# New orders of the work in four phases instead of three, with transpositions placed behind each run of small matmul tiles and each bfloat16 product

## What is computed

```python
x = x + _L0_xattn_ref(_layernorm(x), ctx, ctx, ...)   # 16 heads of 8, softmax over 64 keys
x = x + _L0_ffn_ref(_layernorm(x), ...)               # 8 experts, top 2: relu(x W1 + b1) W2 + b2, weighted
x = x + _L1_xattn_ref(_layernorm(x), ctx, ctx, ...)   # attention without biases
x = x + _L1_ffn_ref(_layernorm(x), ...)
# the last one: c = sigmoid(.) * c + sigmoid(.) * tanh(.) over the 128 sequences as time steps,
# then h = tanh(xt @ wo.T + c_final @ uo.T + bo)
```

## Time and profile before

| | us |
|---|---|
| median of three runs | 842.12 (841.3 to 842.35) |
| the profiled execution | 841.05 |
| its span | 839.2 |
| busy in the span: TensorE matmuls | 820.6 |
| ScalarE | 775.4 |
| VectorE | 775.3 |
| GpSimd | 682.5 |

### The profile page before, as it was taken

How to read it: one execution, slowest core, us unless ns; L and a number is a source line. 1 busy time by engine, 2 the same in 40 slices (tenths; PEclk the granted TensorE clock), 3 DMA queues, 4 the chain that set the end, 5 groups by cost and what they waited for, 6 DMA issues and landing times.

```text
span 839.2 us, 42592 instructions
## 1 busy us (share of the span) xinstructions
PE 820.6 (98%) x15268; PEld 743.5 (89%) x15268; DVE 775.3 (92%) x2778; ACT 775.4 (92%) x2490; POOL 682.5 (81%) x1292
## 2 busy tenths in 40 slices
PE   8899999999999999999999999999999999999996
PEld 5688999999999999999999999999999999998884
DVE  6789999999999999999999999999999999999855
ACT  5899999999999999999999999999999999998874
POOL 5888998888888888888888888888888888887644
PEclk7999999999999999999999999999999999999999
DMA  9400000000000000000000000000000000000005
GB/s 345 175 3 3 2 4 4 4 3 4 3 3 4 4 4 3 4 3 4 3 4 4 4 4 4 3 3 4 3 4 3 4 3 4 4 4 3 3 3 201
DMA packets 6969, 17.74 MB, mean 21 GB/s; under 512 B 752, under 2 KB 2288, under 8 KB 6768
## 3 DMA queue, kind: packets, MB, share of 16 engines
q1 hardware_dynamic: 6336, 14.36, 4.5%
q10 hardware_dynamic: 432, 0.68, 0.3%
HBM read 10.84 MB, written 4.19 MB: 18 GB/s over the span
## 4 chain that ended last, share of the span: by engine, by line
PE 90%; DVE 4%; ACT 3%; issue 2%; POOL 1%; DVEq 0%; POOLq 0%; ACTq 0%
PE ps L458 15%; PE ps L480 13%; PE ps L393 13%; PE ps L378 8%; PE ps L423 7%; PE ps L554 6%; PE ps L540 5%; PE ps L329 4%; PE ps L358 4%; PE ps L437 3%; PE ps L343 3%; PE ps L320 2%; PE ps L404 2%; PE ps L321 2%; PE ps L493 1%
## 5 line engine op out<-in xcount | busy, mean ns | idle before, releaser
L1512 POOL TENSOR_TENSOR h<-Ex 128x512 f32<-128x512 f32 (+1 forms) x144 | 165.9, 1152 | 57.6 <-issue 51.2
L1106 DVE TENSOR_REDUCE mx<-ps 128x8 f32<-128x512 f32 (+1 forms) x288 | 167.0, 620 | 8.2 <-PE ps L378 7.9
L1120 DVE TENSOR_TENSOR Ex<-ps,mx 128x512 f32<-128x512 f32 (+1 forms) x288 | 170.8, 617 | 0.1
L819 ACT ACTIVATE ET<-ps 128x512 f32<-128x512 f32 (+1 forms) x288 | 166.0, 584 | 3.2 <-PE ps L393 2.9
L808 ACT ACTIVATE Ex<-Ex 128x512 f32<-128x512 f32 (+1 forms) x288 | 165.1, 608 | 2.0 <-DVE Ex L1120 1.8
L393 PE MATMUL ps<-w,Ex 128*128 128x128 f32 x1024 | 158.8, 275 | 0.1
L1212 DVE SCALAR_TENSOR_TENSOR acc<-ps,we,acc 128x128 f32<-128x128 f32 x448 | 147.9, 330 | 1.3 <-issue 0.2
L458 PEld LDWEIGHTS ps<-xT,w 128*128 128x128 f32 x1024 | 124.2, 191 | 24.6 <-issue 24.6
L458 PE MATMUL ps<-xT,w 128*128 128x128 f32 x1024 | 144.9, 284 | 0.0
L857 ACT ACTIVATE hT<-ps,w 128x128 f32<-128x128 f32 x512 | 140.1, 398 | 3.1 <-PE ps L458 2.8
L480 PE MATMUL ps<-w,hT 128*128 128x128 f32 x1024 | 139.0, 279 | 0.0
(11 more groups left out here) (108 smaller groups left out, 1847.4 us busy)
## 6 DMA issues: line engine op xcount, KB each, us to landing
cx<-ctx_dram SPq DMA_DIRECT2D x7, 512.0 KB, 12.5
x<-x_dram SPq DMA_DIRECT2D x7, 512.0 KB, 13.1
out_dram<-x SPq DMA_DIRECT2D x14, 256.0 KB, 2.7
w<-weights_dram SPq DMA_DIRECT2D x2, 512.0 KB, 5.4
w<-weights_dram SPq DMA_DIRECT2D x1, 576.0 KB, 8.7
out_dram<-x SPq DMA_DIRECT2D x4, 128.0 KB, 2.6
w<-weights_dram ACTq DMA_DIRECT2D x1, 328.0 KB, 4.4
w<-weights_dram ACTq DMA_DIRECT2D x1, 256.0 KB, 3.1
```

The lines of the kernel that those rows point to most:

```text
L819: e.activation(ET[:, j % 2, r, lo:hi, :, :], b[:, 256 * lo:256 * hi].rearrange("p (c w q) -> p c w q", c=hi - lo, w=2), ACT.Copy).then_inc ...
L1106: e.tensor_reduce(mx[:, j % 2, r, 4 * lo:4 * hi], b[:, 256 * lo:256 * hi].rearrange("p (j k) -> p j k", k=64), AX.X, ALU.max).then_inc(sig ...
L1120: e.tensor_tensor(Ex[:, j % 2, r, 256 * lo:256 * hi].rearrange("p (j k) -> p j k", k=64), b[:, 256 * lo:256 * hi].rearrange("p (j k) -> p ...
L1512: e.tensor_tensor(u, v[:, :, :, 0:32], v[:, :, :, 32:64], ALU.add).then_inc(sig("half1"), 1)
```

## The change

All lags, phases, bank tables and orders are new. There are four phases (rounds -1 to 5, 6 to 11, 12 to 65, 66 to 79) instead of three (0 to 14, 15 to 71, 72 to 79). No operation is added or taken away on any engine, and no shape is changed. VectorE has more waits for its own earlier results (`mv`, `D0` to `D3`, `ri`, `tix`), since the new order would otherwise let a buffer be written anew too soon. `EVEN` is the tile from which empty instructions are strewn between TensorE's products.

```diff
-EVEN = 2
+EVEN = 3
...
-STARTS = (0, 15, 72)
+STARTS = (-1, 6, 12, 66)
...
-       "y1": 3, "e2": 4, "gate": 1, "q": 2, "rt": 4, "turnw": 2, "h0": 2, "sB": 2, "S": 2, "h1": 2, "xin": 1,
+       "y1": 3, "e0": 4, "gate": 1, "turnw": 2, "e1": 4, "h0": 2, "sB": 2, "S": 2, "rt": 4, "h1": 2, "xin": 1,
...
+AHEAD = {"sA": (0, -2, 0, 0), "pv": (1, 0, 0, 0), "e2": (0, 0, 0, -1), "wx0": (4, 3, 2, 0), "q": (0, 0, 0, -1),
...
                     e.wait_ge(sig(f"in_x{chunk[t]}"), 16)
+                if t >= 2:
+                    e.wait_ge(sig("mv"), t - 1)
                 e.bn_stats(st[:, t % 2, 0, :], x[:, t, :]).then_inc(sig("st0"), 1)
...
                 e.wait_ge(sig("xa"), j + 1)
+                if j + L1 >= 2:
+                    e.wait_ge(sig("mv"), j + L1 - 1)
...
                 e.wait_ge(sig("xm"), t + 1)
+                e.wait_ge(sig("mv"), t + L2 - 1)
...
                 e.wait_ge(sig(f"S{r}"), j + 1)
+                if j >= 2:
+                    e.wait_ge(sig(f"D{r}"), j - 1)
...
                 e.wait_ge(sig("half2"), 2 * (j + 1))
+                if j >= 2:
+                    e.wait_ge(sig("ri"), j - 1)
...
                 e.wait_ge(sig("gate"), t + 1)
+                if t >= 2:
+                    e.wait_ge(sig("tix"), t - 1)
```

More of the change, by code:

```diff
@@ L110, in due @@
 def due(i, name):
-    ahead = AHEAD.get(name, (0, 0, 0))
+    ahead = AHEAD.get(name, (0, 0, 0, 0))
     done = max(r + ahead[phase(r)] for r in range(i - 48, i))
@@ L564, in tensor_program @@
                     project_bias()
+                for r in due(i, "y1"):
+                    experts(r, 1)
+                for r in due(i, "e1"):
+                    turn_e(r, 1)
+                for r in due(i, "e3"):
+                    turn_e(r, 3)
+                for r in due(i, "h1"):
+                    hidden(r, 1)
+                for r in due(i, "sB"):
+                    step(r, 1)
+                for r in due(i, "p"):
+                    project(r)
+                for r in due(i, "turnw"):
+                    turn_w(r)
@@ new lines, in tensor_program @@
+                for r in due(i, "wx0"):
+                    out_inputs(r, 0)
+                for r in due(i, "q"):
+                    query(r)
+                for r in due(i, "wx1"):
+                    out_inputs(r, 1)
+                for r in due(i, "gate"):
+                    gate(r)
+                for r in due(i, "sA"):
+                    step(r, 0)
+                for r in due(i, "e2"):
+                    turn_e(r, 2)
+                for r in due(i, "y0"):
+                    experts(r, 0)
@@ new lines, in tensor_program @@
+                for r in due(i, "e0"):
+                    turn_e(r, 0)
+                for r in due(i, "S"):
+                    scores(r)
+                for r in due(i, "turnx"):
+                    turn_x(r)
+                for r in due(i, "xin"):
+                    cell_inputs(r)
+                for r in due(i, "rt"):
+                    turn_r(r)
+                for r in due(i, "kv"):
+                    keys_values(r)
+                for r in due(i, "h0"):
+                    hidden(r, 0)
@@ L937, in scalar_program @@
                     turn_w(r)
+                for r in due(i, "ET3"):
+                    turn_e(r, 3)
+                for r in due(i, "rT"):
+                    turn_r(r)
+                for r in due(i, "ex3"):
+                    exps(r, 3)
                 for r in due(i, "ex2"):
@@ L1034, in scalar_program @@
-                for r in due(i, "kvc"):
-                    keys_values(r)
             e.wait_ge(sig("uo"), 1)
@@ L1264, in vector_program @@
+                for r in due(i, "mx3"):
+                    maxima(r, 3)
+                for r in due(i, "gidx"):
+                    gate_index(r)
                 for r in due(i, "mx2"):
                     maxima(r, 2)
+                for r in due(i, "sb3"):
+                    differences(r, 3)
+                for r in due(i, "c5"):
+                    combine(r, 5)
+                for r in due(i, "sm"):
+                    sums(r)
+                for r in due(i, "c1"):
+                    combine(r, 1)
@@ new lines, in vector_program @@
+                for r in due(i, "c3"):
+                    combine(r, 3)
+                for r in due(i, "aT"):
+                    normal(r)
+                for r in due(i, "sb2"):
+                    differences(r, 2)
+                for r in due(i, "c6"):
+                    combine(r, 6)
+                for r in due(i, "c7"):
+                    combine(r, 7)
+                for r in due(i, "rc"):
+                    inverse(r)
+                for r in due(i, "st2"):
+                    stats_experts(r)
@@ L1266, in vector_program @@
+                for r in due(i, "st0"):
+                    stats_inputs(r)
+                for r in due(i, "c8"):
+                    combine(r, 8)
+                for r in due(i, "xa"):
+                    project(r)
+                for r in due(i, "c4"):
+                    combine(r, 4)
+                for r in due(i, "gtop"):
+                    gate_top(r)
+                for r in due(i, "c0"):
+                    combine(r, 0)
                 for r in due(i, "uB"):
                     update(r, 1)
-                for r in due(i, "mx3"):
-                    maxima(r, 3)
@@ L1270, in vector_program @@
-                for r in due(i, "sb2"):
-                    differences(r, 2)
+                for r in due(i, "st13"):
+                    stats_attention(r)
+                for r in due(i, "ag"):
+                    spread(r)
+                for r in due(i, "gsc"):
+                    gate(r)
+            for i in range(STARTS[1], STARTS[2]):
                 for r in due(i, "sb3"):
@@ new lines, in vector_program @@
+                for r in due(i, "gtop"):
+                    gate_top(r)
+                for r in due(i, "st2"):
+                    stats_experts(r)
+                for r in due(i, "st0"):
+                    stats_inputs(r)
+                for r in due(i, "ag"):
+                    spread(r)
+                for r in due(i, "gidx"):
+                    gate_index(r)
+                for r in due(i, "mx0"):
+                    maxima(r, 0)
+                for r in due(i, "mx2"):
+                    maxima(r, 2)
@@ new lines, in vector_program @@
+                for r in due(i, "mx1"):
+                    maxima(r, 1)
+                for r in due(i, "sb0"):
+                    differences(r, 0)
+                for r in due(i, "sb1"):
+                    differences(r, 1)
+                for r in due(i, "sb2"):
+                    differences(r, 2)
+                for r in due(i, "mx3"):
+                    maxima(r, 3)
+                for r in due(i, "c0"):
+                    combine(r, 0)
+            for i in range(STARTS[2], STARTS[3]):
+                for r in due(i, "sb1"):
+                    differences(r, 1)
+                for r in due(i, "sb2"):
+                    differences(r, 2)
+                for r in due(i, "mx3"):
+                    maxima(r, 3)
+                for r in due(i, "aT"):
+                    normal(r)
+                for r in due(i, "c0"):
+                    combine(r, 0)
+                for r in due(i, "sb3"):
+                    differences(r, 3)
+                for r in due(i, "c1"):
+                    combine(r, 1)
+                for r in due(i, "c2"):
+                    combine(r, 2)
+                for r in due(i, "sm"):
+                    sums(r)
+                for r in due(i, "c3"):
+                    combine(r, 3)
+                for r in due(i, "rc"):
+                    inverse(r)
+                for r in due(i, "c4"):
+                    combine(r, 4)
+                for r in due(i, "xa"):
+                    project(r)
+                for r in due(i, "c5"):
+                    combine(r, 5)
@@ L1307, in vector_program @@
                     combine(r, 8)
+                for r in due(i, "st13"):
+                    stats_attention(r)
                 for r in due(i, "st2"):
                     stats_experts(r)
-                for r in due(i, "uA"):
-                    update(r, 0)
+                for r in due(i, "st0"):
+                    stats_inputs(r)
                 for r in due(i, "gidx"):
@@ L1315, in vector_program @@
                     spread(r)
-            for i in range(STARTS[1], STARTS[2]):
-                for r in due(i, "st2"):
-                    stats_experts(r)
-                for r in due(i, "st13"):
-                    stats_attention(r)
-                for r in due(i, "ag"):
-                    spread(r)
                 for r in due(i, "uB"):
                     update(r, 1)
+                for r in due(i, "mx0"):
+                    maxima(r, 0)
                 for r in due(i, "mx1"):
                     maxima(r, 1)
+                for r in due(i, "mx2"):
```

(14 more changed lines are left out.)

591 lines of the change are left out of this document (302 added, 289 removed), and 86 rows, old and new, of tables (AHEAD, LAG, USES).

## The result

The changed kernel takes 847.9 us (median of 12 runs, 838.95 to 852.4), the kernel before 841.7 in the same comparison (12 runs, 841.14 to 842.35). The ratio is 1.0057, with a 95% interval of 1.0039 to 1.0075: slower by 0.6%, and outside the predicted range. (The two medians give 1.0074; the ratio is taken over the fast runs of each kernel, which leaves out the one of 852.4.) Its runs lie 13 us apart, those of before 1.2. The profiled execution took 845.91, 4.86 more than that of before.

A forecast was written before the change was run, and what follows sets the result against it. TensorE's list bounded the kernel before; afterwards a VectorE-TensorE loop of 12.13 us a round would. 841.05 + 1.6 (54 long rounds) - 0.9 (rounds 66 to 71) = 841.75, plus 1.07 to the median: 842.8 us, range 832.5 to 846.

The forecast's parts named there:

- TensorE's saving: TensorE's list, long phase: new neighbours of `yb`, `turnw` and `S` save 0.145 a round, 12.10 to 11.955 us.
- `yb` and `turnw`: Two bfloat16 products on TensorE: ahead of transpositions instead of ordinary products, each saves some 0.05 us, between 0.03 and 0.06.
- `S`: Run of tiles on TensorE: followed by transpositions (0.055 more) instead of `h1` (0.10 more), it saves 0.045 us.
- The loop: One-round chain, VectorE `c5` to `sb2`, TensorE `e2` to `y1`, back to `c5`: 12.15, taken as 12.13 us, sets the round.
- TensorE half: From the end of `sb2` through `e2`, `y0`, four pieces and `y1` back to `c5`: 4.30 us.
- e2: Transpositions on TensorE, now right behind `yb`: wait for `D2`, the end of `sb2`, and take 0.49 us instead of 0.44.
- VectorE's half: From `c5` to the end of `sb2` on VectorE: 5.49 + 0.52 + 1.84 = 7.85 us.
- the second case: `D2` or `y1` comes some 0.2 earlier, so TensorE's list sets the round: 833.4 us, faster; chance 0.30.
- the four cases: Loop closes (842.8, chance 0.50); loop has slack (833.4, 0.30); added VectorE waits cost time (850.4, 0.12); nothing saved (843.7, 0.08).
- the likeliest case: `c5`-to-`y1` chain sets long-phase rounds at 12.13 us: 842.8 us, 840.0 to 845.5; chance 0.50.
- The fill: First twelve rounds, with orders of their own: change taken as 0, with 2 us either way.
- The end: Rounds 66 to 71, now in the last order, get TensorE's gain: 6 x 0.145, -0.9 us.

The follow-up runs named there:

- the first experiment: The changed kernel with GpSimd's `pw` ahead of the halving sums and `gw` behind `hv1` of the next round: 833.07 us, ratio 0.9897 to the kernel before.

## Why the prediction was wrong

**What bounds the kernel** was right: nothing but TensorE's list set a round before, and the two engines beside it had 0.4 to spare.

**TensorE's saving** was mis-sized: 12.10 - 0.145 = 11.955 was predicted, 11.88 measured, so 0.22. `yb` and `turnw` at some 0.05 each are borne out by rows, and `S` at 0.045 by rows and a run. Missed was the fourth place, `gate`: it stood ahead of a float32 product and now stands ahead of `turnw` and transpositions, 0.075 (`q` at 0.53 instead of 0.45). 0.145 + 0.075 = 0.22.

**The loop** exists as drawn, and its TensorE half was right to the hundredth: from the end of `sb2` to `e2`'s load 0.05, `e2` 0.49, `y0` 0.90, the four pieces 1.76, `y1` 1.06, back to `c5` 0.04, together 4.30. VectorE's half was wrong, and that is **the failed step**: the 7.85 took every busy row of VectorE for work and put waits for GpSimd, which no line of the sum names, at nothing. So it kept a stall that the old order had (0.15) and left out the one that the new order makes (0.57). In a long round this half goes from `c5` to the end of `sb2`:

```profile
615.42 0.74 DVE L1327 SCALAR_TENSOR_TENSOR acc<-ps,we,acc 128x128 f32<-128x128 f32 x2 [0.31 <-PE ps L494]
...
621.67 1.88 DVE L1231 TENSOR_TENSOR Ex<-ps,mx 128x512 f32<-128x512 f32 x3
```

621.67 + 1.88 - 615.42 = 8.13, of which 0.57 is the stall, so 7.56 of work where I had 7.85. The old stretch from `c5` to the first subtraction was put at 5.71 us, of which 0.22 was a wait that falls away: some 0.15 more of it was `nm` waiting for `add_bias`, which the profile books as busy time. The other 0.14 is spread: the stretch from `c5` to `nm` is 0.10 shorter than summed although `gidx`, taken at nothing, takes 0.14 in it; what stands around the old wait at `uB` another 0.06; and the subtractions give 0.04 back. The bare loop is 7.56 + 4.30 = 11.86, just under TensorE's 11.88. With no stall, the second case, "the loop has slack after all", would have come: the 833.07 of the first experiment against its 833.4. I had given it 0.30 only, since no term had room for 0.17 alone; two together had.

**What decided** was in none of the four cases: the loop without slack, and VectorE's wait for GpSimd on it. 11.86 + 0.57 = 12.43, the long rounds. That the likeliest case, 842.8, lies within 1% of the measured time is luck: no round of the long phase took its 12.13. A full long round costs 0.55 more than a short one, and the profiled execution had 25 of them and 6 of 12.23 to 12.25; by that, a median of 847.9 would stand for some (847.9 - 833) / 0.55 = 27 full ones, and the spread of 13 us between runs for some 24 more or fewer. These two are estimates, as only one of the 12 runs left a trace. Why do they come in stretches? In a short round `ve` starts 0.06 before GpSimd's addition, in a long one 0.02 after it. VectorE's list is closed with TensorE in the loop, while `hv0` is released through ScalarE; a round that is late for another reason (a round of 12.25 occurs before too, 3 in 50) moves the one against the other by the 0.08 that is wanted, and each long round leaves it so. The rows fit, but what starts and ends a stretch was not tried, and stays open.

**The sum.** The long phase was taken at +1.6 and gave +5.5 between the thirteenth and the last `kv`, with single rounds 0.2 below and 0.3 above the 12.10. The fill gave -1.3, inside its 2 us either way. The end, taken at -0.9, gave +0.5 and is not explained. The added waits at nothing were right, by the rows of their run; `EVEN` at nothing was not tried alone.

## What to carry to other kernels

An instruction of VectorE that lasts several times as long as its like in other rounds is waiting, though the profile counts it as busy: look at what GpSimd has in flight, before such a row goes into a sum. When orders are moved by tenths of a microsecond, put long GpSimd instructions where VectorE reads PSUM, or behind the small VectorE operation that they need anyway, and don't let the two meet on a chain that closes within a round. And where banks go round in a table, a swap of two pieces must be followed to each piece behind them.

## What the runs showed of the hardware

- A VectorE operation on 128x4 elements (0.15 us) took up to 0.73 with GpSimd's 128x256 addition (0.73) in flight and 0.29 in most rounds with one of half the size; it ended some 20 ns after it. In the changed kernel a lead of 20 ns of that addition was enough; with one of 18, VectorE passed, and the addition took 0.77.
- The form with one tensor operand waited as long (0.73). VectorE's operations with one operand in PSUM do not: the subtractions of 128x512 (line 1231, changed kernel) took 0.68 in the median of 108 that started with a halves' addition in flight and of 116 that did not, none over 0.69.
- A float32 product behind two passes of 8 columns took 0.08 more than in another place (`q` 0.53 against 0.45, `h0` 1.07 against 0.99). Behind the bfloat16 product it took 0.05 more, as predicted.
